# A twelve-layer decoder in one kernel: where the inverse square roots of its normalisations are computed

## The reference

```
def _layernorm(x, axis=-1, eps=1e-05):
    m = jnp.mean(x, axis=axis, keepdims=True)
    v = jnp.var(x, axis=axis, keepdims=True)
    return (x - m) / jnp.sqrt(v + eps)
x = _layernorm(x + layer(x, ...), axis=-1)      # twelve times
```

## Time and profile before

| | us |
|---|---|
| median of three runs | 1800.8 |
| the profiled execution | 1798.09 |
| its span, first to last instruction | 1796.3 |
| PE busy | 1427.7 |
| DVE busy | 1135.3 |
| ACT busy | 729.2 |
| POOL busy | 412.1 |

### The profile page before, as it was taken

How to read it: one execution, slowest core, us unless ns; L and a number is a source line. 1 busy time by engine, 2 the same in 40 slices (tenths; PEclk the granted TensorE clock), 3 DMA queues, 4 the chain that set the end, 5 groups by cost and what they waited for, 6 DMA issues and landing times.

```text
span 1796.3 us, 25705 instructions
## 1 busy us (share of the span) xinstructions
PE 1427.7 (79%) x8738; PEld 936.6 (52%) x8754; DVE 1135.3 (63%) x2697; ACT 729.2 (41%) x1855; POOL 412.1 (23%) x375
## 2 busy tenths in 40 slices
PE   7999756776777556675796638989899899989997
PEld 5777634554455422221464426655566666666664
DVE  5667566664676578888666876655555766654333
ACT  3444424544445445455253513532233444432222
POOL 2233003322323034357410024200100333320000
PEclk9999878998789766768797868979999899999999
DMA  8000000000000400000000000000000000000000
GB/s 326 1 0 1 1 0 1 0 0 1 1 0 0 186 3 1 0 0 0 1 2 1 0 1 1 1 1 0 0 1 2 1 1 1 1 1 1 1 0 12
DMA packets 4202, 24.76 MB, mean 14 GB/s; under 512 B 1168, under 2 KB 3216, under 8 KB 3472
## 3 DMA queue, kind: packets, MB, share of 16 engines
q1 hardware_dynamic: 4112, 23.59, 3.2%
HBM read 23.06 MB, written 0.52 MB: 13 GB/s over the span
## 4 chain that ended last, share of the span: by engine, by line
PE 38%; issue 29%; DVE 16%; POOL 10%; ACT 5%; DVEq 0%; POOLq 0%; DMA 0%; ACTq 0%; SPq 0%
POOL arena L749 6%; PE PS L1234 5%; PE PS L868 5%; PE PS L1219 4%; PE PS L1220 4%; PE PS L843 3%; ACT arena L982 2%; DVE arena L2253 2%; POOL arena L2875 2%; POOL arena L2862 1%; PE PS L832 1%; DVE arena L2244 1%; DVE arena L2200 1%; PE PS L1223 1%; PE PS L195 1%
## 5 line engine op out<-in xcount | busy, mean ns | idle before, releaser
L561 ACT ACTIVATE arena<-PS,arena 128x256 f32<-128x256 f32 (+1 forms) x256 | 112.3, 443 | 175.2 <-DVE arena L659 101.2
L749 POOL TENSOR_TENSOR arena<-arena 128x384 f32<-128x384 f32 (+1 forms) x128 | 119.6, 935 | 243.5 <-DVE arena L669 129.8
L385 PE MATMUL PS<-arena 128*128 128x256 f32 (+1 forms) x512 | 135.3, 367 | 8.3 <-DVE arena L630 4.3
L982 ACT ACTIVATE arena<-PS 128x1024 f32<-128x1024 f32 (+1 forms) x96 | 86.4, 900 | 128.7 <-PE PS L868 128.7
L1322 DVE TENSOR_TENSOR arena<-arena,PS 128x512 f32<-128x512 f32 x82 | 56.4, 688 | 117.1 <-ACT arena L1255 117.0
L2309 POOL TENSOR_TENSOR arena<-arena 128x512 f32<-128x512 f32 x64 | 103.8, 1643 | 90.7 <-DVE arena L2244 36.0
L1255 ACT ACTIVATE arena<-PS 128x512 f32<-128x512 f32 x82 | 49.0, 597 | 165.3 <-PE PS L1220 165.3
L1054 DVE TENSOR_REDUCE arena<-PS 128x4 f32<-128x1024 f32 (+1 forms) x96 | 98.2, 1066 | 28.3 <-PE PS L843 28.3
L2244 DVE TENSOR_TENSOR_SCAN arena<-arena 128x512 f32<-128x512 f32 x64 | 94.0, 1473 | 21.8 <-ACT arena L2141 14.4
L385 PEld LDWEIGHTS PS<-arena 128*128 128x128 f32 x512 | 82.1, 190 | 42.7 <-issue 20.3
L868 PE MATMUL PS<-arena 32*128 32x256 f32 (+1 forms) x768 | 97.0, 371 | 6.9 <-ACT arena L982 3.5
(11 more groups left out here) (423 smaller groups left out, 3318.6 us busy)
## 6 DMA issues: line engine op xcount, KB each, us to landing
w_last<-in_last SPq DMA_DIRECT2D x1, 8260.0 KB, 22.9
w_rest<-in_rest SPq DMA_DIRECT2D x1, 5898.5 KB, 35.5
w_last<-in_first SPq DMA_DIRECT2D x1, 4532.5 KB, 20.2
w_last<-in_first SPq DMA_DIRECT2D x1, 2176.0 KB, 9.2
X<-in_x SPq DMA_DIRECT2D x1, 512.0 KB, 4.5
CT<-in_ctxT SPq DMA_DIRECT2D x1, 512.0 KB, 9.8
out<-X SPq DMA_DIRECT2D x1, 512.0 KB, 3.2
w_consts<-in_consts SPq DMA_DIRECT2D x1, 373.0 KB, 3.2
```

The source lines that it names most:

```text
L385: ins = pe.matmul(PS[:, h % 2, col:col + n], self.QZ[:, h, t * P:(t + 1) * P], keys[:, 0:n], start=True, stop=not masked, skip_group_check ...
L561: ins = a.activation(self.Pr[:, h % 4, col:col + n], PS[:, h % 2, col:col + n], ACT.Exp, bias=self.nm[:, h, t:t + 1], scale=1.0, accum_out ...
L749: g.tensor_tensor(p, p, self.ri[:, h, 0:n].unsqueeze(2).to_broadcast([P, n, w // n]), ALU.mult)\
L982: a.activation(self.PT[:, k:k + 2, :], PS[:, 4:6, 0:2 * n], ACT.Exp).then_inc(self.e_done.sem, 1)
```

## The change

All square roots on ScalarE and the reciprocals after them go. A function `inverse_root` computes a to the power -0.5 on GpSimd, as a tensor_tensor whose second operand is a constant column of -0.5 broadcast. Its result goes where the reciprocal's went (`rs`, `inv`, `rs2`), and the Newton step stays. For the layer normalisations VectorE adds epsilon to the variance in place first, one more operation with a wait of its own, and the Newton step gets epsilon 0. A constant column `power` takes the place of `eps`.

In the order of work: the early group's root stands at the end of the attention layers' GpSimd work, the last group's root in `LayerEnd.gpsimd`, Mamba's at the start of its GpSimd work. In `LocalLayer` the 128x2 root of a batch stands between the second and the third rotation addition of the next batch (for the last batch after all else), and the 128x32 root after the fourth.

```
--- before.py
+++ after.py
@@ -127,6 +126,11 @@
+def inverse_root(g, r, a, power):
...
+    return g.tensor_tensor(r, a, power.to_broadcast(list(a.shape)), ALU.pow)
...
 def refine(link, v, r, a, eps, tmp):
...
@@ -171,22 +175,21 @@
             ins = v.bn_aggr(c.mv[:, n, :], c.bn[:, n, :])
-        ins.then_inc(self.var_ready.sem, 1)
+        c.dve.link(v, ins)
+        v.tensor_scalar(c.mv[:, a:b, 1], c.mv[:, a:b, 1], EPS, None, ALU.add).then_inc(self.var_ready.sem, 1)
...
         c, (a, b) = self.c, self.groups[g]
-        v.wait_ge(self.sd_ready.sem, self.sd_ready.at(0, g + 1))
-        c.dve.link(v, v.reciprocal(c.rs[:, a:b], c.sd[:, a:b]))
-        refine(lambda ins: c.dve.link(v, ins), v, c.rs[:, a:b], c.mv[:, a:b, 1], EPS, c.rt[:, a:b])
+        v.wait_ge(self.rs_ready.sem, self.rs_ready.at(0, g + 1))
+        refine(lambda ins: c.dve.link(v, ins), v, c.rs[:, a:b], c.mv[:, a:b, 1], 0.0, c.rt[:, a:b])
         for n in range(a, b):
...
-    def root(self, a, g):
-        c, (i, j) = self.c, self.groups[g]
-        a.wait_ge(self.var_ready.sem, self.var_ready.at(0, g + 1))
-        a.activation(c.sd[:, i:j], c.mv[:, i:j, 1], ACT.Sqrt, bias=c.eps, scale=1.0)\
-            .then_inc(self.sd_ready.sem, 1)
+    def root(self, g, n):
+        c, (i, j) = self.c, self.groups[n]
+        g.wait_ge(self.var_ready.sem, self.var_ready.at(0, n + 1))
+        inverse_root(g, c.rs[:, i:j], c.mv[:, i:j, 1], c.power).then_inc(self.rs_ready.sem, 1)
...
@@ -213,7 +216,6 @@
             a.activation(c.XT[:, 0:512], c.PS[:, 0, :], ACT.Copy).then_inc(self.x_next.sem, 1)
-        self.root(a, g)
         if not self.last:
...
@@ -223,7 +225,7 @@
     def gpsimd(self, g):
-        pass
+        self.root(g, len(self.groups) - 1)
...
@@ -563,8 +565,6 @@
         def part(it, prev, cur, nxt):
-            if not cur:
-                self.end.root(a, 0)
             for s in range(16):
...
@@ -748,6 +748,7 @@
                     .then_inc(self.pn_done.sem, 1)
+        self.end.root(g, 0)
...
@@ -2094,8 +2095,6 @@
         a.activation(self.A, self.alog, ACT.Exp).then_inc(self.a_ready.sem, 1)
-        a.wait_ge(self.var_ready.sem, self.var_ready.at(0, 1))
-        a.activation(c.sd[:, :], c.mv[:, :, 1], ACT.Sqrt, bias=c.eps, scale=1.0).then_inc(self.sd_ready.sem, 1)
         for i in range(2):
...
@@ -2181,10 +2180,10 @@
             ins = v.bn_aggr(c.mv[:, n, :], c.bn[:, n, :])
-        ins.then_inc(self.var_ready.sem, 1)
-        v.wait_ge(self.sd_ready.sem, self.sd_ready.at(0, 1))
-        link(v.reciprocal(c.rs[:, :], c.sd[:, :]))
-        refine(link, v, c.rs[:, :], c.mv[:, :, 1], EPS, c.rt[:, :])
+        link(ins)
+        v.tensor_scalar(c.mv[:, :, 1], c.mv[:, :, 1], EPS, None, ALU.add).then_inc(self.var_ready.sem, 1)
+        v.wait_ge(self.rs_ready.sem, self.rs_ready.at(0, 1))
+        refine(link, v, c.rs[:, :], c.mv[:, :, 1], 0.0, c.rt[:, :])
         for n in range(T):
...
@@ -2293,6 +2292,9 @@
     def gpsimd(self, g):
+        c = self.c
+        g.wait_ge(self.var_ready.sem, self.var_ready.at(0, 1))
+        inverse_root(g, c.rs[:, :], c.mv[:, :, 1], c.power).then_inc(self.rs_ready.sem, 1)
         c = self.c
...
@@ -2608,10 +2609,6 @@
-        def norms(it, d):
-            a.wait_ge(self.sum_ready.sem, self.sum_ready.at(it, 1, d))
-            a.activation(self.nrm, self.ssq, ACT.Sqrt).then_inc(self.nrm_ready.sem, 1)
...
         def exps(it, k):
...
@@ -2648,9 +2645,6 @@
                 square(it, 1, 1)
-            a.wait_ge(self.var_ready.sem, self.var_ready.at(it, 1))
-            a.activation(self.sd2, self.mv2.rearrange("p (t k) -> p t k", k=2)[:, :, 1], ACT.Sqrt, bias=c.eps, scale=1.0)\
-                .then_inc(self.sd_ready.sem, 1)
             if more:
...
@@ -2658,7 +2652,6 @@
                 square(it, 1, 3)
-                norms(it, 1)
             for f, m in enumerate(self.HID):
...
@@ -2732,8 +2724,7 @@
         def inverses(it, d):
-            v.wait_ge(self.nrm_ready.sem, self.nrm_ready.at(it, 1, d))
-            link(v.reciprocal(self.inv, self.nrm))
+            v.wait_ge(self.root_ready.sem, self.root_ready.at(it, 1, d))
             refine(link, v, self.inv, self.ssq, 0.0, self.nrt)
...
@@ -2804,13 +2795,14 @@
                 ins = v.bn_aggr(self.mv2[:, 2 * t:2 * t + 2], self.st[:, 6 * t:6 * t + 6])
-            ins.then_inc(self.var_ready.sem, 1)
+            link(ins)
+            var = self.mv2.rearrange("p (t k) -> p t k", k=2)[:, :, 1]
+            v.tensor_scalar(var, var, EPS, None, ALU.add).then_inc(self.var_ready.sem, 1)
             if more:
...
                 rotate(it, 1, 2)
-            v.wait_ge(self.sd_ready.sem, self.sd_ready.at(it, 1))
-            link(v.reciprocal(self.rs2, self.sd2))
-            refine(link, v, self.rs2, self.mv2.rearrange("p (t k) -> p t k", k=2)[:, :, 1], EPS, c.rt[:, 0:2])
+            v.wait_ge(self.rs_ready.sem, self.rs_ready.at(it, 1))
+            refine(link, v, self.rs2, self.mv2.rearrange("p (t k) -> p t k", k=2)[:, :, 1], 0.0, c.rt[:, 0:2])
             for t in range(2):
...
@@ -2856,11 +2848,20 @@
     def gpsimd(self, g):
+        def spread_roots(it):
+            g.wait_ge(self.var_ready.sem, self.var_ready.at(it, 1))
+            inverse_root(g, self.rs2, self.mv2.rearrange("p (t k) -> p t k", k=2)[:, :, 1], self.c.power)\
+                .then_inc(self.rs_ready.sem, 1)
...
         def queries_keys(it, d):
             for i in range(4):
+                if d and i == 2:
+                    spread_roots(it)
                 g.wait_ge(self.ab_done.sem, self.ab_done.at(it, i + 1, d))
...
                     .then_inc(self.qk_sum.sem, 1)
+            g.wait_ge(self.sum_ready.sem, self.sum_ready.at(it, 1, d))
+            inverse_root(g, self.inv, self.ssq, self.c.power).then_inc(self.root_ready.sem, 1)
             g.wait_ge(self.inv_ready.sem, self.inv_ready.at(it, 1, d))
...
@@ -2887,6 +2888,7 @@
         probabilities(B - 1)
+        spread_roots(B - 1)
```

More of the change, by code:

```diff
@@ L149, in __init__ @@
         self.var_ready = c.sig("var_ready", len(self.groups), 1)
-        self.sd_ready = c.sig("sd_ready", len(self.groups), 1)
+        self.rs_ready = c.sig("rs_ready", len(self.groups), 1)
         self.x_tile = c.sig("x_tile", T, 1)
@@ L2678, in scalar @@
         value(0, 0, 2)
-        norms(0, 0)
         with a.Fori(0, B - 1) as it:
@@ L2923, in constants @@
     return [("ident", np.eye(P, dtype=f)), ("headmask", headmask),
-            ("eps", np.full((P, 1), EPS, f)), ("one", np.ones((P, 1), f)),
-            ("onehot", (i[:, None] % 32 == np.arange(32)[None, :]).astype(f)), ("band", band), ("own", own), ("keep", 1.0 - spare), ("unit", unit), ("fall", fall), ("iota", iota),
+            ("one", np.ones((P, 1), f)),
+            ("onehot", (i[:, None] % 32 == np.arange(32)[None, :]).astype(f)), ("band", band), ("power", np.full((P, 1), -0.5, f)), ("own", own), ("keep", 1.0 - spare), ("unit", unit), ("fall", fall), ("iota", iota),
             ("iota8", np.broadcast_to(np.arange(8, dtype=f), (P, 8)))]
@@ L3036, in build @@
         c.W = W
-        c.ident, c.eps, c.one = W("ident"), W("eps"), W("one")
+        c.ident, c.power, c.one = W("ident"), W("power"), W("one")
         onehot = c.sb("onehot", [P, 32], BF16)
```

49 lines of the change are left out of this document (21 added, 28 removed).

## The result

The changed kernel took 1845.6 us (median of 4 runs, 1841.8 to 1848.3) against 1801.0 for the kernel before (4 runs): a ratio of 1.0246, 95% interval 1.0225 to 1.0267. It is slower, as forecast, but by 45 us where 14 were forecast, and outside the range that went to 1843. The profiled execution of the changed kernel took 1841.8 us, with a span of 1839.9 (+43.6) and nearly the same mean granted clock, 0.873 for 0.875.

What follows compares the result with a forecast made beforehand. No engine was full (PE 79%, DVE 63%), so a chain passing from engine to engine was taken as the bound. Terms -11.0 + 17.8 + 7.2 = +14.0 us gave 1815 us against the median, range 1797 to 1843.

Steps and rivals of the forecast that it cites:

- the power: GpSimd's power at 23 exposed roots, 334 elements: 40 ns an element plus 0.19 us fixed, 17.8 us in all.
- X8: Time of one power at the 8 exposed wide roots, eight elements in a row: 0.51 us.
- X2: Time of one power at the 7 exposed two-wide roots: 0.27 us.
- Y: Time of one power at the 8 query and key norms, 128x32: 1.47 us, all on the path.
- The upper bound: Power cost from above: sixty passes of 1.66 ns, 100 ns an element, 33 us.
- rival C: Power far dearer than 60 passes, some 350 ns an element: +117 us, 1918; chance 0.11.
- rivals A and B: A: power cheap as a multiply, 1802, chance 0.12. B: also no added collision, faster, 1795, chance 0.15.
- The places: Roots exposed at 8 wide, 7 two-wide and 8 norm places; spread roots in looped batches and early groups at zero.
- The loads: Few table loads in the open: two routers gain 2.6 us together, the second local layer's first norm 1.35.
- rival D: Table loads placed by block, so the router's 2.6 us stay: 1817, counted inside the forecast (0.62 together).
- The collision: POOL's clearings and tables against DVE's multiplies at three narrow attentions: 5.5 us for two, 1.7 for the third, together 7.2.
- The sum: Whole kernel: -11.0 fixed gains, +17.8 power, +7.2 collision, +14.0 us.

Runs made afterwards that it cites:

- the clearings late: Changed kernel with GpSimd's two clearings of the narrow attentions held until the X transposes are evicted: 1837.7 us, ratio 1.0180 to the kernel before.
- The two delays: Kernel before with two or six unread VectorE reciprocals added at the layer end at 868 us: 1806.9 and 1799.9 us.
- the hold: Kernel before with GpSimd's tables and clearings at the three narrow attentions waiting for the layer end's last root, roots still on ScalarE: 1799.6 us, ratio 0.9983.
- the late clearing: Kernel before with only the second clearing (3.52 us) held until the X transposes are evicted: 1795.1 us, ratio 0.9959.
- its two versions with a delay: Kernel before with the second clearing late plus six or three unread VectorE reciprocals at the 868 us layer end: 1791.6 and 1797.8 us.
- the delay of two: Kernel before with two unread VectorE reciprocals of 96 columns added at the layer end at 868 us: 1806.9 us, ratio 1.0024.
- the delay of six: Kernel before with six unread VectorE reciprocals of 96 columns added at the layer end at 868 us: 1799.9 us, ratio 0.9989.
- the version with three reciprocals: Kernel before with the second clearing late and three unread VectorE reciprocals at the 868 us layer end: 1797.8 us, ratio 0.9974.

## Why the prediction was wrong

**The step that failed** is the power: "I take 24 passes, 40 ns an element, an estimate whose number of passes is my choice". It measured 157 ns an element and 0.38 fixed, so X8, X2 and Y were 1.64, 0.70 and 5.42 us, not 0.51, 0.27 and 1.47. With 8, 7 and 8 exposed calls that is 13.1 + 4.9 + 43.4 = 61.4 us for the 17.8 of the sum: 43.6 too few. The upper bound failed as well: sixty passes at a multiply's speed, 100 ns, was meant as a bound and was a second guess. No row showed a power, and rival C, at 350 ns, was too dear by a factor of 2.2. The list of exposed calls did not depend on the size, so it held. The sign did depend on it (rivals A and B had a cheap power and came out level or faster), and a dearer power only made it surer.

**The places** were right. Y on the path in full: 5.54 us of DVE idle time each, and half the elements gave back 19.7 us. Wide and two-wide roots exposed, 6-wide roots hidden: idle 1.8, 0.8 and 0.1. For the eight 128x2 roots of the local layers DVE waits 1.6 us in all, which the two last batches account for at 0.8 each; those in the loop stay hidden, as forecast. The handover from DVE to POOL is the 0.08 of the forecast at 18 of the 23 exposed roots (the addition ends at 909.79, the power starts at 909.87) and 0.17 at five of the eight wide ones (258.21 and 258.38); POOL to DVE is 0.03 where 0.08 was taken.

**The loads** went where the forecast said, rival D is refuted, and the router's wait shrank by 1.28. With the powers made cheap, the local layers came out 5.9 us shorter from 257 to 612, so the gains were real: the forecast had 7 x 0.53 + 1.35 + 2 x 0.21 + 0.24 = 5.7 there, before a call on POOL was paid. Eleven exposed multiplies there, of about 0.2 us each, should have taken some 2 us of it back. TensorE stood at its lower clock for 82 us of this stretch, for 98 in the kernel before, which may be why they did not; no run tests it.

**The collision** was right as a row, 5.39 us where "about 5.4" stood, twice. At L3a its term had the wrong sign, -1.0 for +1.7, because POOL's tables, which read SBUF, held a Newton step by 0.2 us at most. The size of the +5.5 for the other two stays open. Of the 3.35 and 3.2 us by which the stages that end with these multiplies grew, the powers explain 2.8 and 1.4, so 0.5 and 1.8 are left for the collision, where 2.7 each stood; taking the clearings away shortened these stages by 1.0 and 1.7 us in the one profile, but the median of four runs by 7.9. The narrow attentions right behind are 3.7 and 3.4 us shorter than before. That is not the collision's own time coming back, since with the clearings late they are just as short. It is TensorE's clock: the low stretches of 10 us at 886 and 1182 of the kernel before are gone. The two delays show that a shift alone takes away the first, -3.6 and -3.5 with no power in the kernel. The second is gone as well in the hold, in the late clearing and in its two versions with a delay, which have no power either and pass that stage in 93.7 to 94.5 us, where the changed kernel takes 94.5. That the shift alone did it there is not shown.

**The sum** with the measured powers: -11.0 + 61.4 + 7.2 = +57.6, against +43.6 measured. Of the missing 14 us, 7.1 lie in the two narrow attentions (-3.7 and -3.4 up to their early groups, where nothing was forecast), 3.7 in the stage that ends at L2f (forecast 1.4 for the power, 1.7 for the tables and -1.3 for the router, +1.8; measured -1.9), and 2.1 and 0.9 in the stages that end with the colliding multiplies (forecast 5.5 and 4.1; measured 3.35 and 3.2). Of the 3.7, 2.7 are the tables' sign; the rest of these I can't settle. The kernel with the hold, which has the 2.38 us multiplies at L2f and the old roots, shows -2.3 in that stage too, and the delay of two shows -1.5 with nothing changed there. The term that the prediction lacks altogether is TensorE's clock: stages that it had taken as fixed move by 3.7 us down to 15 us up with the same matmuls in them.

**What is open.** What decides whether the low stretch behind 868 lasts 0, 10, 34 or 44 us. PE idles at the layer end before it, for longer where something delays the multiplies: in the kernel with the delay of six it is busy 6.6 of the 16 us from 868 on, and no low stretch follows; in the one with the late clearing it is busy 13.9 of the 16 us from 870 on, and a low stretch of 34 us follows. Two kernels do not make a rule, and the version with three reciprocals, with its low stretch of 44 us at 960 instead, speaks against a simple one. Open too is how much of the 7.9 us of the late clearings is the collision.

## What to carry to other kernels

An operation that no row of the profile shows must be priced per element by a measurement, or its bounds taken so wide that they hurt: here 334 elements on the path turned a factor of four into 44 us. Before moving a short operation to an idle engine, ask how long that engine takes for one element, not how idle it is; 128x2 was nearly harmless, 128x32 was not. And where TensorE's granted clock changes inside a stage, treat a gain or loss under about ten us as unproven until the stage's clock is the same in both profiles, and test it with a pure delay. A median between two groups of runs is the time of neither.

## What the runs showed of the hardware

- GpSimd's power of two float tiles: 0.38 us a call and 157 ns an element of a row, from five sizes (0.70 us for 128x2 to 5.42 for 128x32), within 2 ns in three more kernels. A multiply of 128x16 on the same engine took 0.22 us.
- A longer delay made a kernel faster: with 4.7 us of idle work at one layer end it took 1799.9 us, with 1.6 us of it 1806.9. In the second narrow attention behind it, 60 us with PE busy for 58 or 59 had a granted clock of 1.00 with the longer delay and 0.81 with the shorter.
- In 28 stages of 890 matmuls or so the length followed the time at a granted clock of 0.50: 93.7 to 95.3 us with 5.5 to 7.5 us of it, 97.7 to 98.0 with 15.9 to 19.4, 108.5 to 108.8 with 40.3 to 40.6, and 113.1 with 48.6.
- One program (the kernel before with a late clearing) took 1789 to 1790 us in five runs, at a mean granted clock of 0.881 to 0.882, and 1800 to 1804 in five others, at 0.873 to 0.878.
- Eight normalising multiplies of VectorE took 2.14 us alone, 5.22 to 5.44 beside GpSimd's clearing, and 2.38 beside GpSimd's tables. The Trainium skill ("SBUF — State Buffer", Who interferes with whom) has VectorE's two-port modes and any GpSimd operation lock each other out for a whole instruction. The clearing agrees, with 5.39 us; beside the tables, with 2.38, it hardly shows.
